# A two-block windowed attention kernel: which pair of windows shares a bank's partition halves

## What is computed

```
y = layer_norm(x, ln1_g, ln1_b)                        # block 1: y rolled by (-3, -3)
wins = windows of y                                    # (16 images * 16 windows, 49, 64)
q, k, v = split(wins @ qkv_w + qkv_b)                  # 8 heads, head size 8
attn = q @ k.T * 8 ** -0.5 + bias_tab[REL_IDX] + mask  # mask: block 1 only
out = softmax(attn, axis=-1) @ v
x = x + out @ proj_w + proj_b
z = gelu(layer_norm(x, ln2_g, ln2_b) @ fc1_w + fc1_b)
x = x + z @ fc2_w + fc2_b
```

## Time and profile before

| | before |
|---|---|
| median of 3 runs | 834.54 us (830.64 to 839.32) |
| the profiled execution | 833.86 us, of which span 832.1 |
| TensorE busy | 733.5 us (88%), 15798 matmul records |
| VectorE busy | 520.2 us (63%) |
| ScalarE busy | 360.6 us (43%) |
| GpSimd busy | 202.4 us (24%) |
| matmuls of the head scores (kexp and qexp) | 8192 records, 139.8 us busy |
| of pv | 4096 records, 61.5 us |
| of f_v (wv) | 1024 records, 37.4 us |
| of proj (wph) | 128 records, 50.5 us |
| attention steps | about 60 to 340 us and 440 to 700 us |

### The profile page before, as it was taken

How to read it: one execution, slowest core, us unless ns; L and a number is a source line. 1 busy time by engine, 2 the same in 40 slices (tenths; PEclk the granted TensorE clock), 3 DMA queues, 4 the chain that set the end, 5 groups by cost and what they waited for, 6 DMA issues and landing times.

```text
span 832.1 us, 35518 instructions
## 1 busy us (share of the span) xinstructions
PE 733.5 (88%) x15798; PEld 488.5 (59%) x15798; DVE 520.2 (63%) x917; ACT 360.6 (43%) x628; POOL 202.4 (24%) x503
## 2 busy tenths in 40 slices
PE   3867899999999998999759999999999997999878
PEld 2634676677667765343336676667767653333658
DVE  2643896788677765787555776677667463784123
ACT  1512445445444444675324454444534454574300
POOL 4000022122113101346400221123112111799000
PEclk9967999999999999999978999999999999999959
DMA  9200111112112111000001211112111111000004
GB/s 238 34 20 21 41 58 56 56 56 64 49 52 66 53 47 45 22 1 1 20 21 35 61 57 46 46 55 69 51 55 61 53 32 44 0 2 2 2 19 136
DMA packets 47661, 38.44 MB, mean 46 GB/s; under 512 B 28564, under 2 KB 46996, under 8 KB 47508
## 3 DMA queue, kind: packets, MB, share of 16 engines
q1 hardware_dynamic: 46496, 33.96, 14.2%
q10 hardware_dynamic: 1012, 2.20, 0.8%
HBM read 18.47 MB, written 4.01 MB: 27 GB/s over the span
## 4 chain that ended last, share of the span: by engine, by line
PE 41%; DVE 5%; issue 3%; DMA 1%; ACT 0%; POOL 0%; SPq 0%; DVEq 0%; POOLq 0%; ACTq 0%
PE psum L1017 41%; DVE nmax L805 1%; PE psum L1412 1%; DMA dpk<-osb 1%; DVE lt L784 0%; DVE XW L904 0%; DVE ly L790 0%; DVE lt L783 0%; DVE lt L789 0%; DVE kexp L989 0%; DVE lt L788 0%; DVE ly L786 0%; DVE ly L781 0%; ACT lv L483 0%; DVE kexp L991 0%
## 5 line engine op out<-in xcount | busy, mean ns | idle before, releaser
L415 POOL TENSOR_TENSOR att<-osb,rec 128x392 f32<-128x392 f32 x64 | 70.8, 1107 | 417.4 <-DMA rec<-dens 408.0
L805 DVE TENSOR_REDUCE nmax<-psum 113x16 f32<-113x784 f32 x128 | 118.7, 969 | 83.1 <-PE psum L1017 83.1
L524 ACT ACTIVATE pt<-psum 113x784 f32<-113x784 f32 x128 | 98.6, 822 | 112.6 <-PE psum L1017 110.8
L1017 PE MATMUL psum<-bt,dup_r 113*113 113x392 f32 x256 | 101.0, 394 | 2.6 <-DVE rx L821 1.4
L1017 PE MATMUL psum<-rx,sel_r 128*113 128x392 f32 x256 | 87.7, 343 | 0.0
L1017 PE MATMUL psum<-kexp,qsb 32*49 32x98 f32 x4096 | 71.8, 258 | 8.1 <-issue 7.4
L1017 PEld LDWEIGHTS psum<-kexp,qsb 32*49 32x49 f32 x4096 | 55.9, 121 | 27.2 <-issue 26.2
L1017 PE MATMUL psum<-qexp,ksb 32*49 32x98 f32 x4096 | 68.0, 251 | 0.7 <-issue 0.5
L831 DVE RECIPROCAL rpk<-dpk 64x49 f32<-64x49 f32 x64 | 28.9, 452 | 62.5 <-DMA dpk<-osb 62.4
L1017 PE MATMUL psum<-pt,vbd 113*32 113x49 f32 x4096 | 61.5, 209 | 6.0 <-ACT osb L531 3.1
L1017 PEld LDWEIGHTS psum<-qexp,ksb 32*49 32x49 f32 x4096 | 53.5, 117 | 19.4 <-issue 19.0
(11 more groups left out here) (173 smaller groups left out, 1222.2 us busy)
## 6 DMA issues: line engine op xcount, KB each, us to landing
rec<-dens SPq DMA_DIRECT2D x64, 196.0 KB
kexp<-ksb SPq DMA_DIRECT2D x128, 49.0 KB
qexp<-qsb SPq DMA_DIRECT2D x128, 49.0 KB
XW<-x_dram SPq DMA_DIRECT2D x14, 196.0 KB, 4.8
out_dram<-XW SPq DMA_DIRECT2D x14, 196.0 KB, 2.4
dpk<-osb SPq DMA_DIRECT2D x64, 12.2 KB
dens<-rpk SPq DMA_DIRECT2D x64, 12.2 KB, 2.1
pt<-w_dram ACTq DMA_DIRECT2D x2, 384.0 KB, 6.8
```

The source lines that it names most:

```text
L415: nc.gpsimd.tensor_tensor(att[:, 4 * part:4 * part + 4, :], osb[part][:, :].rearrange("p (a n) -> p a n", a=4), rec[part][:, :].rearrange( ...
L524: nc.scalar.activation(pt[grp][:, b:b + 2, :], SC[0:KROWS, b:b + 2, 0:BANK], ACT.Exp)\
L805: nc.vector.tensor_reduce(nmax[:, GWIN * grp:GWIN * grp + GWIN, :].rearrange("p w (g a) -> p a w g", g=2)[:, b:b + 2], SC[0:KROWS, b:b + 2 ...
L1017: return nc.tensor.matmul(o, a, b, start=start, stop=stop, **k)
```

## The change

The score banks now hold on their partition halves two neighbouring windows of the same image pair instead of the same window of the two images. Both images of a window stand side by side in the columns (4 x 49 = 196).

- `head_scores`: for each pair x of windows and each member i, four products (h4) of 196 columns; 16 in a group instead of 32.
- `f_v`: `wv2` becomes a 128 x 128 matrix with the weights of each image on its diagonal block; 8 products of 128 rows and 128 columns, the members i on the partition halves.
- `proj`: the outputs of window members lie on other rows of `att`; 8 products (member i, half hh of the heads, image w) of 128 rows and 64 stationary columns with 196 moving columns instead of 2 of 392.
- The bias: the two members of a pair now need different masks on the two halves. The column mask goes to four extra rows of the product (`BROWS` = 53, `BIASR` = 117): `rows_r` replaces `dup_r`, and the table's rows 49 to 52 hold -100 where a token class is masked. The block 1 tables have two pairs instead of four windows, and are broadcast.
- The selection matrices (`slot`, `sel`) and `nmaxw` follow the new place of the row maxima. GpSimd sets two more tiles to zero at the start.

```diff
+BROWS = NTOK + 4
+BIASR = 64 + BROWS
...
-                wv2=sb(f"wv2{k}", [128, CH]),
+                wv2=sb(f"wv2{k}", [128, 128]),
...
-                bn=sb(f"bn{k}", [KROWS, 2 * k + (1 - k), 2, GWIN if k else 1, 2 * NTOK], F32R),
-                bt=sb(f"bt{k}", [KROWS, 2 * k + (1 - k), TILES4, GWIN if k else 1, 2 * NTOK], F32R)))
+
+                bn=sb(f"bn{k}", [BIASR, 1 + k, 2, 1 + k, 2 * NTOK], F32R),
+                bt=sb(f"bt{k}", [BIASR, 1 + k, TILES4, 1 + k, 2 * NTOK], F32R)))
...
             if table == "bn":
-                rows, h4 = slice(64 * (h4 % 2), 64 * (h4 % 2) + NTOK), h4 // 2
+                rows, h4 = slice(64 * (h4 % 2), 64 * (h4 % 2) + BROWS), h4 // 2
+            n = rows.stop - rows.start
             if blk:
-                return t[rows, 1 if odd and grp else 0, h4, :, :]
-            return t[rows, 0, h4, :, :].to_broadcast([rows.stop - rows.start, GWIN, 2 * NTOK])
+                return t[rows, 1 if odd and grp else 0, h4, :, :].rearrange("p x (a m) -> p x a m", a=1)\
+                    .to_broadcast([n, GWIN // 2, 2, 2 * NTOK])
+            return t[rows, 0, h4, :, :].to_broadcast([n, GWIN, 2 * NTOK])
...
-                nc.vector.tensor_scalar(p["wv2"][:, :], raw[:, 2 * CH:3 * CH], v[:, G1:G1 + 1], None, ALU.mult)
+                for w in range(2):
+                    r = slice(CH * w, CH * w + CH)
+                    nc.vector.tensor_scalar(p["wv2"][r, r], raw[r, 2 * CH:3 * CH], v[r, G1:G1 + 1], None, ALU.mult)
...
             def table(k, t):
 
-                p = P[k]
-                wins = slice(3 * (t % 2), 3 + t % 2) if k else slice(0, 1)
-                n = wins.stop - wins.start
-                bn, bt = p["bn"][:, t // 2, :, wins, :], p["bt"][:, t // 2, :, wins, :]
-
-                def windows(a, rows, banks=TILES4):
-                    return a.rearrange("p (a b m) -> p a b m", a=banks, b=1).to_broadcast([rows, banks, n, 2 * NTOK])
+                p, variant, pair = P[k], t // 2, t % 2
+                bn, bt = p["bn"][:, variant, :, pair, :], p["bt"][:, variant, :, pair, :]
 
                 def heads(a, h=HEADS):
                     return a.rearrange("p (h m) -> p h m", h=h)
 
+                def banks(a, h=TILES4):
+                    return a.rearrange("p (a m) -> p a m", a=h)
+
                 few = btmp[:, 0:BANK // 2]
                 tlink(nc.vector.tensor_tensor(heads(few, 4), heads(tabn[k][:, :], 4),
-                                              maskn[:, t:t + 1, :].to_broadcast([KROWS, 4, NTOK]), ALU.add))
-                tlink(nc.vector.tensor_copy(bn, windows(few, KROWS, 2)))
+                                              maskn[:, t:t + 1, :].to_broadcast([BIASR, 4, NTOK]), ALU.add))
+                tlink(nc.vector.tensor_copy(bn, banks(few, 2)))
                 tlink(nc.vector.tensor_tensor(heads(btmp[:, :]), heads(tabt[k][:, :]),
-                                              maskt[:, t:t + 1, :].to_broadcast([KROWS, HEADS, NTOK]), ALU.add))
-                tlink(nc.vector.tensor_copy(bt, windows(btmp[:, :], KROWS)))
-                tlink(nc.vector.tensor_tensor(bt[64:KROWS], windows(btmp[64:KROWS, :], NTOK), bt[64:KROWS].bitcast(F32),
-                                              ALU.subtract))
+                                              maskt[:, t:t + 1, :].to_broadcast([BIASR, HEADS, NTOK]), ALU.add))
+                tlink(nc.vector.tensor_copy(bt, banks(btmp[:, :])))
+                tlink(nc.vector.tensor_tensor(bt[64:BIASR], banks(btmp[64:BIASR, :]), bt[64:BIASR].bitcast(F32), ALU.subtract))
...
-                    nc.vector.tensor_scalar(nmaxw[:, :, w, :], nmax[:, :, :], wmask[:, w:w + 1], None, ALU.mult)\
+                    nc.vector.tensor_scalar(nmaxw[:, :, w, :], nmax[:, :, :].rearrange("p (x w) h -> p x (w h)", w=2), wmask[:, w:w + 1], None, ALU.mult)\
...
             def f_v(p, buf):
 
-                for w in range(WIN):
-                    for im in range(2):
-                        r = slice(64 * im, 64 * im + 64)
-                        last = mm(bA[64 * im:64 * im + NTOK, w * CH:(w + 1) * CH],
-                                  z[buf][r, w * NTOK:(w + 1) * NTOK], p["wv2"][r, :])
+                for x in range(WIN // 2):
+                    for i in range(2):
+                        last = mm(bA[64 * i:64 * i + NTOK, 128 * x:128 * (x + 1)],
+                                  z[buf][:, (2 * x + i) * NTOK:(2 * x + i + 1) * NTOK], p["wv2"][:, :])
                 last.then_inc(v_ready, 1)
 
             def head_scores(still, moving, grp):
 
-                for win in range(GWIN):
-                    cols = slice((GWIN * grp + win) * NTOK, (GWIN * grp + win + 1) * NTOK)
-                    for h4 in range(TILES4):
-                        r = slice(32 * h4, 32 * h4 + 32)
-                        for w in range(2):
-                            last = mm(SC[64 * w:64 * w + NTOK, h4, 2 * NTOK * win:2 * NTOK * (win + 1)],
-                                      still[r, cols], moving[r, 2 * w:2 * w + 2, cols], False, win == GWIN - 1)
+                for x in range(GWIN // 2):
+                    for i in range(2):
+                        win = GWIN * grp + 2 * x + i
+                        cols = slice(win * NTOK, (win + 1) * NTOK)
+                        for h4 in range(TILES4):
+                            r = slice(32 * h4, 32 * h4 + 32)
+                            last = mm(SC[64 * i:64 * i + NTOK, h4, 4 * NTOK * x:4 * NTOK * (x + 1)],
+                                      still[r, cols], moving[r, :, cols], False, x == GWIN // 2 - 1)
                 return last
...
-                    mm(SC[0:KROWS, h4, 0:BANK], dup_r[64 * (h4 % 2):64 * (h4 % 2) + NTOK, 0:KROWS], bias_of(p, "bn", blk, odd, grp, h4),
+                    mm(SC[0:KROWS, h4, 0:BANK], rows_r[64 * (h4 % 2):64 * (h4 % 2) + BROWS, 0:KROWS], bias_of(p, "bn", blk, odd, grp, h4),
...
-                    mm(SC[0:KROWS, h4, 0:BANK], dup_r[0:KROWS, 0:KROWS], bias_of(p, "bt", blk, odd, grp, h4), True, False)
+                    mm(SC[0:KROWS, h4, 0:BANK], rows_r[0:BIASR, 0:KROWS], bias_of(p, "bt", blk, odd, grp, h4), True, False)
...
             def proj(p, g, bank=bA):
 
                 pe.wait_ge(att_done, 2 * g + 2)
-                for hh in range(2):
-                    last = mm(bank[:, 0:TOK], p["wph"][:, hh, :], att[:, :, hh * NTOK:(hh + 1) * NTOK], hh == 0, hh == 1)
+                for i in range(2):
+                    for hh in range(2):
+                        for w in range(2):
+                            last = mm(bank[64 * w:64 * w + 64, 0:TOK].rearrange("p (x i n) -> p x i n", i=2, n=NTOK)[:, :, i],
+                                      p["wph"][:, hh, 64 * i:64 * i + 64], att[:, w::2, hh * NTOK:(hh + 1) * NTOK],
+                                      hh == 0, hh == 1)
                 last.then_inc(proj_ready, 1)
...
+    pair, rest = np.divmod(np.arange(128), 4 * HEADS)
+    odd, rest = np.divmod(rest, 2 * HEADS)
     rw, rh = np.divmod(rest, HEADS)
     at = np.arange(2 * GWIN)
-    c["slot"] = ((win[:, None] % GWIN == at // 2) & (rh[:, None] // TILES4 == at % 2)).astype(f)
+    c["slot"] = (4 * (pair[:, None] % 2) + 2 * rw[:, None] + rh[:, None] // TILES4 == at).astype(f)
     sel = np.zeros((128, 2 * TILES4, 128), f)
     for p in range(128):
-        sel[p, TILES4 * (win[p] // GWIN) + rh[p] % TILES4, 64 * rw[p]:64 * rw[p] + NTOK] = 1
+        sel[p, TILES4 * (pair[p] // 2) + rh[p] % TILES4, 64 * odd[p]:64 * odd[p] + NTOK] = 1
...
+    rows = np.zeros((128, 128), f)
+    maskn = np.zeros((BIASR, 4, NTOK), f)
     for w in range(2):
-        maskn[64 * w:64 * w + NTOK] = m
-        maskt[64 * w:64 * w + NTOK] = m
-    c["maskn"], c["maskt"] = maskn.reshape(KROWS, -1), maskt.reshape(KROWS, -1)
+        for o in range(2):
+            rows[64 * w + np.arange(NTOK), 64 * o + np.arange(NTOK)] = 1
+        maskn[64 * w:64 * w + NTOK, 2:] = -100 * row[:, None, :]
+        for k in range(4):
+            at = 64 * w + NTOK + k
+            rows[at, 64 + np.arange(NTOK)] = (low == k // 2) & (right == k % 2)
+            maskn[at, 1] = -100 * (right != k % 2)
+            maskn[at, 3] = -100 * ((low == k // 2) & (right != k % 2))
+    c["rows"] = rows
```

44 lines of the change are left out of this document (22 added, 22 removed).

## The result

| | before | after |
|---|---|---|
| median | 832.59 us (829.73 to 839.32, 4 runs) | 792.95 us (789.98 to 793.14, 4 runs) |
| profiled span | 832.1 us | 791.1 us |
| ratio | | 0.9505, 95% interval 0.944 to 0.957 |
| TensorE busy | 733.5 us | 711.6 us |
| TensorE idle in the span | 98.6 us | 79.5 us |

The changed kernel is faster, by 39.6 us, where 26 were forecast. The span shrank by 41.0 us: 21.9 of TensorE's busy time and 19.1 of its idle time.

The account below looks back on a forecast made before the run. TensorE was taken to bound the attention steps, outrunning its instruction supply in a dense stretch. TensorE's terms summed to -28.9 us, the SyncE ring added +3, so 833.86 - 26 = 808 us, range 796 to 824.

Parts of the forecast that it names:

- head groups: Head-score groups on TensorE: half the products at equal columns, 0.96 to 0.84 us each, 128 times, -15.4 us.
- f_v: The f_v products on TensorE: 16 of 64 columns become 8 of 128, 32 times, -0.5 us.
- proj: The proj products on TensorE: a shape changeover and an open first load add 0.14 us, 32 times, +4.5 us.
- supply, marked: TensorE's marked issue idle, read as late instruction fetch: 18 of the 21.0 us should go, -18 us.
- supply, slow groups without a note: TensorE groups slowed by late instructions without marked idle: a few us possible, left out of the sum.
- ring: SyncE's cycle of spreads, gather, dens out and rec back: late in a third of steps by 0.3 us, +3 us.
- constants: The load of constants grows from 1384 to 1520 columns, +0.5 us.
- the supply term: TensorE outruns its instruction fetch in the dense stretch; fewer instructions should remove nearly all stalls, -18 us, ends 0 and -21.
- Rival B: On TensorE all gains arrive, unmarked slow groups vanish too and nothing becomes late: 797 us, chance 0.11.
- Rival C: SyncE's ring binds at 15.9 us a step, so only 17 us are gained: 817 us, chance 0.13.
- D: TensorE's stalls are not instruction supply and stay: only -11 us, 823 us, chance 0.08.
- E: Weight loads of full-height column halves stay open in proj and f_v, +20 us: 828 us, chance 0.06.

Follow-up runs that it names:

- experiment 2: Changed kernel, head-score products cut into two of 98 columns in the earlier tile order: all groups 827.3 us, windows 0 to 3 alone 811.2, windows 4 to 7 alone 804.0.
- experiment 5: Changed kernel with one or three further 12 KB transfers a step on the SyncE queue ahead of the kexp spread: 805.7 and 930.3 us.
- windows 0 to 3 cut: Changed kernel with only the head-score products of windows 0 to 3 cut into two of 98 columns, in the earlier tile order: 811.2 us.
- the kernel with three transfers: Changed kernel with three further 12 KB SyncE transfers a step ahead of the kexp spread, each waiting for the one before: 930.3 us.

## Why the prediction was wrong

Against the span, -41.0 us, by the prediction's own terms:

| term | put | measured | from |
|---|---|---|---|
| head groups | -15.4 | -15.9 | 0.96 to 0.84 us, 128 times |
| f_v | -0.5 | -0.3 | with bn 1.57 to 1.56, 32 times |
| proj | +4.5 | +3.0 | +0.09 behind xl (22 times), +0.05 ahead of bn (26 times), -0.06 four times |
| pv ahead of a bias product | 0 | +2.2 | 0.86 to 0.93 us, 30 times |
| supply, marked | -18 | -21.0 | the issue row, gone |
| supply, slow groups without a note | 0 | -8.3 | the dense stretch beyond its pace, 10.0 to 1.7 |
| ring | +3 | +1.7 | row-max wait, 6.4 to 8.1 |
| constants | +0.5 | not seen apart | |
| rest | | -2.4 | not settled |

**The step that failed is the supply term**: "I take 18 of the 21.0 us", with the groups slowed without an idle note left out of the sum and given "a few us" below its end. It measured -29.3 in all. Rival B had this at -8 more and the time within 4 us (797), and got a chance of 0.11. The evidence was at hand: one packet of instructions ahead of the 1.47 us of idle time in the earlier trace rows stands a slow group of 1.38 us, and the same shortage shows as the one and as the other. The 8.3 us are read from both traces, part of them as 5.2 us of busy time of the head groups beyond pace and 1.7 of pv, whose instructions did not change; and with the instructions of experiment 2 (all cut) the 8.3 us came back.

**The ring** was put at +3 from one slow landing in the earlier trace rows, with the fear that it would be slow at both places in a third of the steps. In the changed kernel a cycle is this long:

```profile
117.23 2.43 SPq L285 DMA_DIRECT2D kexp<-ksb  x4
131.53 2.42 SPq L285 DMA_DIRECT2D kexp<-ksb  x4
146.52 2.42 SPq L285 DMA_DIRECT2D kexp<-ksb  x4
```

14.30 and 14.99 us, around TensorE's 15.03. The 14.82 of the earlier trace rows was no lower bound for it. It was right that the ring is next, as experiment 5 shows; it does not set the step yet. Rival C is out.

**Right**: the pace of all three reshaped products to 0.01 or 0.02 us, down to the 0.14 of `proj`. Two of its small sums are off as written and change nothing: 0.96 - 0.80 - 0.084 is 0.08, not 0.09, and 16 x 0.056 less 8 x 0.109 over 32 steps is 0.8 us for `f_v`, not 0.5. And it counted the 0.14 for all 32 `proj`, where the 0.09 stands 22 times and the 0.05 26 times, and did not see pv change its pace. The reading that 196-column products remove the slow second half of a group held. Packets (92) and issue idle (none listed, "under 3") came as written. D (the stalls are not supply) is out by experiment 2, and E (loads left open in full-height column halves) by `proj`: from xl's start to bn it is 1.75 us (125.40 to 127.15), exactly the 0.18 + 1.57 that the forecast gave; E asked for 0.18 + 2.0. The rule that the prediction cites of the Trainium skill lets a weight load overlap matmuls in flight only when the row group differs; all eight products of `proj` have the same row group, and their loads are hidden. The same section of the Trainium skill also has loads pulled ahead when they go to a background weight buffer; that would fit, and no run here tests it.

## What to carry to other kernels

Where a stall ends on "nothing that the profile shows" and cuts groups in the middle, count instructions over that stretch, and add to the marked idle time what groups of the same kind take beyond their median: in this kernel that was 8.3 us beside 21.0, and with windows 0 to 3 cut 5.7 beside 3.2. Then set the ends of the idle pieces beside the ends of the instruction queue's packets. An experiment that changes the number of instructions must keep their order over the tiles; order alone cost 0.27 us a group here, 34 us of pace, of which 17 showed in the time (844.8 against 827.3), since the slower groups met less idle time for nothing. A term that is named as "a few us below the end" belongs in the sum.

## What the runs showed of the hardware

- Order over tiles: 64 records of 98 columns on eight tiles take 0.96 us with two records of a tile side by side, 1.23 with four; `proj` 1.48 with the column halves alternating, 2.20 with one half ahead of the other.
- `proj` with one half ahead of the other: the second half starts while records of the first, ahead of it in the program, still wait; 10 of its 16 records start in the first 1.21 us.
- The number of instruction pairs costs time beyond each group's own pace, at equal columns: 20.6 us between 321 and 449 pairs a step.
- TensorE's idle time for nothing ends 1.20 to 1.55 us behind the end of a packet of its instructions, 29 times of 29 in the kernel before, and comes at whole multiples of 127 records.
- After a wait of 3.2 us inside a step the granted clock was 0.50 for the next 5 us, so a wait costs more than its length: idle of TensorE for kexp and row maxima was 96 us in the kernel with three transfers (61.5 and 34.9) against 9 in after, and the time rose by 137.
